# Sorted feed-forward projection: pacing the indirect transfers by the turned tiles

## The reference, cut to what matters

```python
x = x + 0.5 * ffn(layernorm(x))        # feed-forward 1
x = x + attention(layernorm(x))        # 16 heads, not touched here
x = x + 0.5 * ffn(layernorm(x))        # feed-forward 2, same weights

def ffn(xn):
    q, k, v = fff(xn, q_params), fff(xn, k_params), fff(xn, v_params)
    return softmax(q @ k.T / 16) @ v

def fff(xn, ...):                      # per token: walk a tree of depth 4, then
    leaf = walk(xn)                    # one of 16 leaves,
    return relu(xn @ w1[leaf] + b1[leaf]) @ w2[leaf] + b2[leaf]   # 256 -> 64 -> 256
```

## Time and profile before

| what | us |
|---|---|
| median of 3 runs (3543.06 to 3554.68) | 3553.56 |
| the profiled execution's own time | 3545.07 |
| its span in the profile | 3543.4 |
| PE busy in the span | 2965.5 (84%) |
| DVE busy | 2119.5 (60%) |
| ACT busy | 1785.6 (50%) |
| POOL busy | 795.3 (22%) |

### The profile page before, as it was taken

The page is one execution under the profiler, slowest core; times in us unless marked ns, Lnnn a source line. Parts: engine busy times, 40 slices in busy tenths (PEclk is TensorE's granted clock), DMA queues, the critical chain, the costliest instruction groups (busy, mean ns, idle before and its releaser), DMA issues. The chain is left out here.

```text
span 3543.4 us, 54686 instructions
## 1 busy us (share of the span) xinstructions
PE 2965.5 (84%) x20622; PEld 1771.0 (50%) x20622; DVE 2119.5 (60%) x3299; ACT 1785.6 (50%) x3479; POOL 795.3 (22%) x1400
## 2 busy tenths in 40 slices
PE   4158689999688999999999999999674157689999
PEld 2046578888343333333333333333341046578888
DVE  4023345544347899999999999995244023345554
ACT  3024334333121788888888888888342034333333
POOL 1721321000013122222222222211021722221000
PEclk7578789999795999999999999999897578799999
DMA  9447511010557454444444455440324347411100
GB/s 285 150 143 223 163 48 41 28 32 22 190 204 87 47 64 56 56 57 56 56 56 56 60 61 61 55 51 9 107 97 103 127 150 227 151 44 41 32 27 23
DMA packets 455582, 314.03 MB, mean 89 GB/s; under 512 B 166859, under 2 KB 430032, under 8 KB 455328
## 3 DMA queue, kind: packets, MB, share of 16 engines
q1 hardware_dynamic: 421408, 226.66, 31.8%
q0 software_dynamic: 33920, 83.93, 7.4%
HBM read 183.16 MB, written 130.97 MB: 89 GB/s over the span
## 5 line engine op out<-in xcount | busy, mean ns | idle before, releaser
L1414 DVE TENSOR_REDUCE mx_ha<-s_ps_ha 128x2 f32<-128x1024 f32 x1024 | 1242.6, 1221 | 109.7 <-PE s_ps_ha L1321 104.9
L1479 ACT ACTIVATE probs_ha<-s_ps_ha 128x512 f32<-128x512 f32 x2048 | 1109.0, 595 | 223.3 <-PE s_ps_ha L1332 90.7
L1321 PE MATMUL s_ps_ha<-ks_ha,qs_ha 48*128 48x512 f32 x2048 | 763.7, 456 | 18.7 <-DMA ks_ha<-parts_d 13.2
L1332 PE MATMUL s_ps_ha<-qs_ha,ks_ha 50*128 50x512 f32 x2048 | 753.4, 448 | 0.9 <-ACT probs_ha L1479 0.2
L1343 PE MATMUL o_ps_ha<-probs_ha,vs_ha 128*32 128x256 f32 (+1 forms) x7936 | 652.0, 401 | 21.5 <-DVE oT_ha L1441 21.5
L1321 PEld LDWEIGHTS s_ps_ha<-ks_ha,qs_ha 48*128 48x128 f32 x2048 | 315.7, 191 | 455.4 <-DVE mx_ha L1414 358.2
L413 DVE COPY y_p<-y_ps_p 128x256 f32<-128x256 f32 x282 | 119.5, 424 | 463.0 <-remote 296.7
L836 ACT ACTIVATE probsT_a<-pT_ps_a 128x512 fp32r<-128x512 f32 x256 | 146.4, 597 | 424.4 <-PE pT_ps_a L709 424.4
L1343 PEld LDWEIGHTS o_ps_ha<-probs_ha,vs_ha 128*32 128x32 f32 x7936 | 156.9, 108 | 383.1 <-issue 182.1
L1332 PEld LDWEIGHTS s_ps_ha<-qs_ha,ks_ha 50*128 50x128 f32 x2048 | 307.5, 186 | 32.7 <-ACT probs_ha L1479 32.2
L529 PE MATMUL h_ps_p<-xsT_p,wa_p 128*65 128x128 f32 x1128 | 186.9, 291 | 114.2 <-issue 92.4
(11 more groups left out here) (188 smaller groups left out, 3919.1 us busy)
## 6 DMA issues: line engine op xcount, KB each, us to landing
xs_p<-xs_d SPq DMA_DIRECT2D x66, 512.0 KB
ys_d<-y_p SPq DMA_DIRECT2D x66, 512.0 KB
qs_ha<-parts_d SPq DMA_DIRECT2D x192, 128.0 KB, 6.2
ks_ha<-parts_d SPq DMA_DIRECT2D x192, 128.0 KB, 7.0
parts_d<-parts_hp POOLq DMA_DIRECT2D x32, 512.0 KB, 3.2
xs_d<-y_p SPq DMA_DIRECT2D x15, 1024.0 KB, 10.8
leaf_w_p<-in_wa SPq DMA_DIRECT2D x6, 1040.0 KB
leaf_w_p<-in_wb SPq DMA_DIRECT2D x6, 1040.0 KB
```

Source lines behind the costliest of these rows:

```text
L1321: nc.tensor.matmul(s1_ps[:, e % BANKS, :], qs[0:QKROWS, n % SLOTS, c, :], ks[0:QKROWS, n % SLOTS, g * 4:(g + 1) * 4, :].rearrange("p c t - ...
L1332: nc.tensor.matmul(out, ks[LOW:LOW + KR, n % SLOTS, c, :], qs[LOW:LOW + KR, n % SLOTS, g * 4:(g + 1) * 4, :].rearrange("p c t -> p (c t)") ...
L1414: nc.vector.reduce_max(mx[:, at:at + 2], s1_ps[:, e % BANKS:e % BANKS + 2, :], AX_X).then_inc(s1_free, 1)
L1479: nc.scalar.activation(probs[:, (n + c) % (LATE + 1), g * 512:(g + 1) * 512], s2_ps[:, turn % TURNS, :], ACT.Exp).then_inc(s2_free, 1)
```

## The change: waits for turned tiles before the indirect transfers

```diff
             for k, f in enumerate(ORDER):
                 ...
                 pool.wait_ge(slot_step, 3 * (k + 1))
                 for t in range(GT):
+                    if k >= 1:
+                        pool.wait_ge(turned, t + 1 if k == 1 else GT + 2 + 3 * t // 2)
                     pool.indirect_dma_start(xs_d[f], ..., xn[:, t, :], None).then_inc(scattered[f], 16)
             ...
             for i, f in enumerate(ORDER[:2]):
                 for k in range(YB):
                     pool.wait_ge(y_stored[k], ...)
                 for t in range(QT):
+                    pool.wait_ge(turned, (i + 2) * SEG - 12 + t if i == 0 else 2 * SEG + 4 + 2 * t)
                     dst = ...
                     pool.indirect_dma_start(dst, None, ys_d[f], ...).then_inc(early_rows, 16)
```

## The result

The changed kernel takes 3370.36 us (median of 4 runs, 3369.85 to 3375.13), the kernel before 3554.12 us on the same chip (4 runs, 3543.06 to 3558.25): ratio 0.9491, 95% interval 0.9468 to 0.9514, 184 us less. The forecast was 3373 us. The profiled execution took 3370.2 us with a span of 3368.5 (before 3545.1 and 3543.4).

What follows compares the result with a forecast made beforehand. A backlog of POOL's indirect transfers delays PE's signals. Excess 4 + 16 + 0 + 8 + 0 + 3 = 31 us per feed-forward, 62 instead of 242.6, saves 180.6: 3553.6 - 180.6 = 3373 us, range 3325 to 3440.

Steps and rivals of the forecast that it cites:

- The excess: Both feed-forward tile loops, time over 1.20 us a tile: 242.6 us lost before, 62 left after, 180.6 saved.
- Start and second scatter: First tiles at half clock, 4 us of excess; then 32 tiles with one transfer each at 1.70 us, 16 us.
- Third scatter: One transfer each 1.5 tiles, slower than the 1.41 us drain, so no backlog: excess 0, upper bound 45 us.
- First gathers: 16 tiles with one gather each, same mix as the second scatter: excess 8 us instead of 14.8.
- Second gathers: One gather in two tiles (2.4 us): excess 0 instead of about 15 us.
- Rest: Remaining restarts and field changes in each feed-forward: 3 us of excess.
- Deadlines of the row loads: Second and third scatters end before the next field's first row load is asked for, so no new wait.
- Rival (a), the clock stays low: PE stays at half clock, 2.13 us a tile beside transfers: time 3503, in half measure 3415; chance 0.22.
- Rival (b), each transfer holds the signals wherever it stands: Each of 96 paced transfers costs its 1.41 us drain without overlap: 41 us slower, 3595; chance 0.05.
- Rival (c), the change does nothing: POOL may not make signals late; a start-up trouble of the tile loop would leave 3554 us; chance 0.03.
- Rival (d), full overlap at 3331: Lower bounds everywhere, excess 10 us per feed-forward, 223 saved, time 3331; chance 0.12 with beyond.
- The rule of DVE's copies locking POOL out: fp32 DVE copies within SBUF block POOL's descriptor writing, losing some 20 us over both feed-forwards; left out of the sum.

Runs made afterwards that it cites:

- experiment 2: Changed kernel with the early gathers issued back to back again, only the scatters waiting: 3438.32 us, 0.9703 of the kernel before.
- experiment 1: Changed kernel with the second and third scatters issued back to back again, only the gathers waiting: 3504.79 us, 0.9891 of the kernel before.
- Experiment 4: Changed kernel with the third field's leaf weights loaded in eight pieces, one behind each of eight group stores: 3351.22 us, 0.9463 of the kernel before.
- experiment 3: Changed kernel with the waits grouped so that four transfers go back to back, same mean rate: 3416.86 us, 0.9645 of the kernel before.
- experiment 10: Changed kernel with the waits grouped so that eight transfers go back to back: 3501.07 us, 0.9864 of the kernel before.
- experiment 6: Kernel before, with plain POOL transfers to consecutive rows replacing the indirect ones of the second and third scatter: 3406.9 us beside 3548.5.
- experiment 5: Kernel before, with the second and third scatter moving 64 of 256 columns of each row: 3542.8 us beside 3548.5.
- experiment 9: Changed kernel, with the second and third scatter moving 64 of 256 columns of each row: 3360.1 us beside 3547.3 for the kernel before.
- experiment 11: Kernel before on chip 13, with a POOL memset of 256 floats a row before each transfer of the second and third scatter: 3332.24 us, 0.9989.

## Why the prediction was right, and where its terms were not

Forecast 3373 us, measured 3370.4; against the profiled execution 3364.5 was worked out, and 3370.2 came. The forecast case (even transfers, most of the excess gone) is what happened. By its steps:

- *The excess*, 242.6 us before, 62 forecast: measured 201.4 - 169.2 = 32.2 in each feed-forward, 64.4 in all.
- *Start and second scatter*, forecast 4 + 16 = 20. The first y copy comes at 135.9, some 2.7 us late (3.9 less one tile of 1.2), and the next 33 intervals take 50.0 us, 10.4 over 39.6: 13 in all. A tile took 1.5 us and not 1.70. The middle of 1.27 and 2.13 was too high: the clock stood at 0.96 from 137 us on, so the 2.13 us tile at half clock, from which the upper value was taken, never held for long. The reason given for the middle, that it is nearer the row of three tiles in 3.2 us, does not choose it: a middle is as near to either value.
- *Third scatter*, forecast 0: between y copies 33 and 81 there are 71.8 and 72.8 us for 57.6, so 14 to 15 over. 7.8 and 9.4 of these are the gap at tile 55 (intervals of 8.99 and 10.61, less 1.2), the rest some 6 us, 0.2 per transfer. **The missed term is the leaf load.** It was in the kernel before, issued at 274 us between the same stores, but tiles stood still there anyway, under the first gathers from 277.8 us. The prediction put the whole 14.8 us of the earlier trace rows down to these gathers. They cost at least that much alone (18.9 us in experiment 2, with no leaf load near), but the gap costs 6.6 and 7.9 us alone too (experiment 1, with no transfer of POOL near). The step that failed is "excess 0" for the third scatter: it gave the tiles back a stage from which a cover had been taken away, without listing what else was issued under it. The 6 us beside the gap speak against the same step in another way: at one transfer in 1.8 us, slower than the drain of 1.41, the backlog should have cost nothing. Experiment 4, without the gap, has them too (63.1 and 62.7 us for 57.6).
- *First gathers*, forecast 8: 24.2 and 22.7 us for 19.2, so 5 and 3.5. *Second gathers*, forecast 0: 39.5 and 39.1 for 38.4, about 1.
- *Rest*, forecast 3: the last intervals are 1.3 us under 1.20 a tile.

So each feed-forward's sum is right to 1 us (31 and 32.2) while its parts are off by -7, +14, -4, +1 and -4. The missed gap and the terms set too high cancel; that the total came so near is luck. That most of the excess goes when the transfers are spread is not: experiments 1, 2, 3 and 10 bring it back where they are bunched again.

- *Deadlines of the row loads.* None was missed. After the first tile PE waits for rows once in the whole loop, which is the gap (waits of PE from 134 us to the end of the loop):

```profile
PE xT_ps_p L509 <- DMA xs_p<-xs_d: 6.1, 1, 6.1
```

- *Rival (a), the clock stays low:* fell. It is 0.96 from 137 us on in the second scatter, and 1.00 in the stages from 184.8 and from 282 us (one transfer per 1.5 and per 2 tiles).
- *Rival (b), each transfer holds the signals wherever it stands:* fell for spaced transfers (0.33 us each against the 1.19 from which it decides), but long bursts come near its 1.41 us: 1.2 each at 16 in a row, which is why the kernel before was so slow.
- *Rival (c), the change does nothing:* fell by the result and by experiments 1 and 6 (the tiles stand when the scatters are bunched again, and run when their form alone is changed). The rule that was set against it, the Trainium skill, "SBUF — State Buffer", section "SBUF: two separate sides", that PE waits on nobody and transfers don't contend with compute, holds here for the bytes (experiments 5 and 9 move a quarter of them and lose the same in those stages). For the signals, of which that section does not speak, the traces decide otherwise: with indirect transfers in a row PE's next engines stand still, beside plain ones they don't (experiment 6).
- *Rival (d), full overlap at 3331:* the changed kernel does not reach it. With the leaf load in pieces and more even waits it is 3346.6.
- *The rule of DVE's copies locking POOL out* (same section), by which some 20 us would be lost: L269's transfers take 954 ns at least and 960 in the median, over all 96 and over the 64 that now go beside tiles alike; before it was 959 and 963. The traces do not show it.
- *26 ns a signal* (the Trainium skill, "TensorE: Matmul & The Clock Gate", section "The cost: per-tile semaphore tail"): the lateness of 30 us in the earlier trace rows stays unexplained by it. What in an indirect transfer holds PE's signals was not found. What is measured runs from PE's start of a group to the consumer's start; the ends of matmuls are modelled in the profile.

What the prediction said would show it was there: y copies 1.5 us apart in the first 32 tiles, the scatters over 167 us, a loop of some 200 us. Its "no wait before a y copy over 4 us" failed in one place per feed-forward, the gap at tile 55, and its "near 1.20 in the next 48" is 1.3 with the gap aside.

## What to carry to other kernels

When POOL issues a series of indirect transfers beside a tile loop whose engines hand over by PE's signals, look at the interval between tiles while they run; if it grows, spread them over the tiles, one in 1.25 to 2 where the deadlines allow, and singly: here eights in a row gave back 131 of 184 us, fours 47. Price a stall by what stays when it is gone: list every transfer that is issued inside it, for a weight load that it hid will stand alone afterwards; cut into pieces behind the stores, it left no gap here. Measure the kernel before on more than one chip: here a stall worth some 5% was there on two and not on a third.

## What the runs showed of the hardware that was not expected

- Only signals of PE are seen late, by some 30 us, and only beside indirect transfers of POOL and for 12 us behind them: 5 tiles in 88 us with them, but PE busy 23.84 of 28 us beside plain ones that are issued more than twice as fast (0.54 against 1.27 us). Why this is so, and why chip 13 is free of it, stays open.
- Their number counts and not their bytes: a quarter of the bytes leaves 88 us of stall (4 tiles) at a DMA share of 0.11.
- The price grows with the length of a burst: in the second scatter 0.33, 0.38 and 0.88 us per transfer for 1, 4 and 8 in a row, over the whole loop 0.2, 0.5 and 0.9, and 1.2 for 16 gathers, where the prediction drew the drain at 1.41 us and no price for transfers spaced wider than that.
- It depends on the chip: the kernel before takes 3547 us on chip 9, 3549 on chip 1 and 3333 on chip 13, and there (experiment 11) the tiles come each 1.25 us beside 16 gathers in a row.
- A weight load of 2 x 1040 KB in one piece holds later stores of the same queue, so that DVE waits 8.2 and 9.8 us for one, at a DMA share of 1.08; in eight pieces it costs nothing that can be seen.
